# Reading two PSUM banks with one operation: exponentials of one head and row maxima of the other

## The reference, cut to what matters

```python
qkv = (x @ w_qkv.T + b_qkv).reshape(b, n, 3, H, D).transpose(2, 0, 3, 1, 4)
q = _apply_rope(jax.nn.elu(q) + 1.0, sin, cos)
k = _apply_rope(jax.nn.elu(k) + 1.0, sin, cos)
attn = jnp.einsum('bhnd,bhmd->bhnm', q, k) * scale
attn = jax.nn.softmax(attn, axis=-1)
attn_out = jnp.einsum('bhnm,bhmd->bhnd', attn, v)
...
x = _layernorm(x + attn_out + lepe)      # lepe: a depthwise convolution of v along n
h = relu(s0 * concat([x, -x]) @ sign(k0)) * 2
h = relu(s1 * h @ sign(k1)) * 2
x = _layernorm(x + s2 * h @ sign(k2))
```

## Time and profile before

| | us |
|---|---|
| median of 3 runs | 2167.17 |
| lowest and highest | 2163.6 and 2169.74 |
| the profiled execution | 2168.84 |
| its span from first to last instruction | 2166.8 |
| busy in the span: PE, DVE, ACT, POOL | 2077.0, 1696.8, 1499.5, 1008.6 |

### The profile page before, as it was taken

How to read it: one execution, slowest core, us unless ns; L and a number is a source line. 1 busy time by engine, 2 the same in 40 slices (tenths; PEclk the granted TensorE clock), 3 DMA queues, 4 the chain that set the end, 5 groups by cost and what they waited for, 6 DMA issues and landing times.

```text
span 2166.8 us, 43669 instructions
## 1 busy us (share of the span) xinstructions
PE 2077.0 (96%) x17136; PEld 836.7 (39%) x17136; DVE 1696.8 (78%) x3094; ACT 1499.5 (69%) x2867; POOL 1008.6 (47%) x578
## 2 busy tenths in 40 slices
PE   4899999999999999999999999999999999999988
PEld 2123333344433434334343443434343343434345
DVE  7978998787887887878787887878878788877143
ACT  3299888766777667776777767776677766767532
POOL 2849269432866157472584427761475704300000
PEclk8689999999999999999999999999999999999999
DMA  5101200010010200111001200002001110000000
GB/s 179 33 9 37 82 19 26 26 67 21 16 34 20 89 16 9 35 58 49 16 25 26 83 25 17 28 16 96 11 17 36 31 57 16 16 9 28 1 1 39
DMA packets 40428, 76.87 MB, mean 35 GB/s; under 512 B 15024, under 2 KB 19488, under 8 KB 37280
## 3 DMA queue, kind: packets, MB, share of 16 engines
q1 hardware_dynamic: 35040, 51.02, 8.2%
q0 software_dynamic: 5184, 23.07, 2.8%
HBM read 46.27 MB, written 25.17 MB: 33 GB/s over the span
## 4 chain that ended last, share of the span: by engine, by line
PE 79%; DVE 13%; ACT 5%; issue 2%; DMA 0%; POOL 0%; SPq 0%; POOLq 0%; ACTq 0%; DVEq 0%
PE unit_banks L723 25%; PE unit_banks L587 21%; PE o_bank L632 19%; DVE maxima L987 8%; PE unit_banks L736 5%; PE unit_banks L659 4%; ACT probs L814 3%; PE unit_banks L597 2%; PE unit_banks L647 1%; DVE hT L1056 1%; DVE h0T L1059 1%; DVE stats L1133 1%; PE unit_banks L640 0%; ACT work L856 0%; ACT work L855 0%
## 5 line engine op out<-in xcount | busy, mean ns | idle before, releaser
L987 DVE TENSOR_REDUCE maxima<-unit_banks 128x1 f32<-128x512 f32 x2048 | 1307.4, 684 | 326.2 <-PE unit_banks L587 321.3
L814 ACT ACTIVATE probs<-unit_banks 128x512 f32<-128x512 f32 x2048 | 1118.7, 599 | 540.3 <-PE unit_banks L597 536.5
L587 PE MATMUL unit_banks<-k_stack,q_stack 48*128 48x512 f16 x2048 | 660.3, 392 | 26.0 <-DVE maxima L987 22.4
L597 PE MATMUL unit_banks<-q_stack,k_stack 50*128 50x512 f16 x2048 | 657.3, 387 | 6.3 <-ACT probs L814 4.2
L632 PE MATMUL o_bank<-probs,v_pair 128*32 128x256 f32 x8192 | 565.4, 388 | 0.5
L723 PE MATMUL unit_banks<-h0T,w 128*128 128x512 f16 x2048 | 480.1, 380 | 0.0
L1385 POOL TENSOR_TENSOR attn<-o_rows_sb,rden 128x256 f32<-128x256 f32 x63 | 39.2, 622 | 787.9 <-DVE rden L1000 774.3
L587 PEld LDWEIGHTS unit_banks<-k_stack,q_stack 48*128 48x128 f16 x2048 | 155.1, 94 | 525.9 <-DVE maxima L987 273.5
L632 PEld LDWEIGHTS o_bank<-probs,v_pair 128*32 128x32 f32 x8192 | 207.5, 109 | 297.0 <-issue 216.9
L723 PEld LDWEIGHTS unit_banks<-h0T,w 128*128 128x128 f16 x2048 | 189.4, 98 | 222.8 <-issue 33.1
L597 PEld LDWEIGHTS unit_banks<-q_stack,k_stack 50*128 50x128 f16 x2048 | 155.5, 93 | 46.3 <-ACT probs L814 37.0
(11 more groups left out here) (148 smaller groups left out, 1664.0 us busy)
## 6 DMA issues: line engine op xcount, KB each, us to landing
rows<-in_x POOLq DMA_DIRECT2D x8, 1024.0 KB, 5.9
q_stack<-q_scratch SPq DMA_DIRECT2D x128, 64.0 KB, 2.0
k_stack<-k_scratch SPq DMA_DIRECT2D x128, 64.0 KB, 2.0
work<-in_xT SPq DMA_DIRECT2D x7, 1024.0 KB, 6.9
q_scratch<-parts POOLq DMA_DIRECT2D x14, 512.0 KB, 3.3
k_scratch<-parts POOLq DMA_DIRECT2D x14, 512.0 KB, 3.2
out<-rows SPq DMA_DIRECT2D x7, 1024.0 KB, 4.9
q_stack<-q_scratch SPq DMA_DIRECT2D x128, 32.0 KB, 1.9
```

What stands on the lines that cost most here:

```text
L587: nc.tensor.matmul(units.out(unit), q_stack[row:row + STACK, r, t * P:(t + 1) * P], k_stack[row:row + STACK, r, half * 512:(half + 1) * 51 ...
L597: nc.tensor.matmul(units.out(unit), k_stack[row:end, r, kt * P:(kt + 1) * P], q_stack[row:end, r, half * 512:(half + 1) * 512], start=True ...
L814: nc.scalar.activation(probs[:, 2 * (kt % 2) + h, half * 512:(half + 1) * 512], units.out(unit), ACT.Exp, scale=exp_regs[2 * (n % PAIRS) + ...
L987: nc.vector.reduce_max(maxima[:, v // T % 2, h * T + t, half:half + 1], units.out(unit), AXIS_X)\
```

## The change

ACT reads both halves of T(s,1,·) with one exponential of 1024 columns. It waits for the second half to be full, and frees both banks at its end. DVE does the same for the row maxima of S(v,0,·) where the two banks are neighbours in the right order: with the ring (0, 1) that is always so, and with the ring (0, 1, 4) in every third step. The exponentials of head 0 and the row maxima of head 1 stay as they were, and so do the row maxima ahead of the step loop.

```diff
+            def exp_both_halves(s, h):
+                n, kt = divmod(s, T)
+                first, last = (("T", s, h, half) for half in range(2))
+                units.wait_full(act, last)
+                if h == 1:
+                    wait(act, pv_done, 2 * (s - 2) + 2)
+                banks = slice(units.bank[first], units.bank[first] + 2)
+                nc.scalar.activation(probs[:, 2 * (kt % 2) + h], units.psum[:, banks].rearrange("p b n -> p (b n)"), ACT.Exp,
+                                     scale=exp_regs[2 * (n % PAIRS) + h]).then_inc(units.free_sem(first), 2)
...
-                for half in range(2):
-                    exp_probs(s, 1, half)
+                exp_both_halves(s, 1)
...
+            def row_max_both_halves(v, h):
+                t = v % T
+                first, last = (("S", v, h, half) for half in range(2))
+                if units.bank[last] != units.bank[first] + 1:
+                    for half in range(2):
+                        row_max(v, h, half)
+                    return
+                units.wait_full(dve, last)
+                banks = slice(units.bank[first], units.bank[first] + 2)
+                nc.vector.reduce_max(maxima[:, v // T % 2, h * T + t, :], units.psum[:, banks], AXIS_X)\
+                  .then_inc(units.free_sem(first), 2)
...
-                    for half in range(2):
-                        row_max(v, 0, half)
+                    row_max_both_halves(v, 0)
```

## The result

The changed kernel takes 2248.89 us (median of 4 runs, 2245.91 to 2259.46) against 2168.11: a ratio of 1.0385, 95% interval 1.0365 to 1.0404, or 81 us more. I had forecast 2230, range 2188 to 2262. The profiled execution took 2248.41 us with a span of 2246.3, 79.5 us more than before.

What follows compares the result with a forecast made beforehand. PE, busy 96% of the span, was taken to bound the kernel. Batch terms 20.6 + 10.1 + 24 + 3.9 + 4.2 = 62.8 us on 2168.84 gave 2231.6, less 1.7 for the median: 2230, range 2188 to 2262.

Steps and rivals of the forecast that it cites:

- Free steps: Steps without a dealt piece: 3.16 us against 2.49 in the first batch, 3.46 against 2.85 in the second.
- plain L1 steps: Steps with a long dealt piece: gap 2.41 us against the 1.93 needed, so nothing lost.
- the first batch: Its 49 free steps, where the T ring of two banks decides: 20.6 us more.
- Durations: Wide operations of 1024 columns: row maximum 1.22 us (ends 1.15 and 1.37), exponential 1.05 us (0.98 and 1.20).
- The small terms of the third to seventh batch: Scale, hT, L0, elu, V, statistics and bound steps: 4.8 us a batch, 24 for five.
- steps with two L0 units: Third to seventh batch, DVE already late: nine steps, each 0.2 us later, 1.8 us a batch.
- the steps around elu: Third to seventh batch, elu on ACT: cycle 3.46 to 3.97 us, PE's work covering two thirds; eight steps, 1.4 us together.
- V, statistics, bound: Third to seventh batch, where the wide operation's end, 0.15 us later, reaches the next S: 0.7 us a batch.
- The clock: Rival: PE's clock falls in the new free steps, 0.44 us more a cycle, 28 us, 2258; chance 0.15.
- the eighth batch: Six free steps at about 0.35 us, L0 steps 1.8, the rest 0.3: 4.2 us more.
- That saved overhead pays: Rival: fewer, wider operations shorten the ACT and DVE part of the chain, 6 us faster, 2161; chance 0.05.
- Half the price: Rival: ACT's and DVE's lateness already hides more of the free steps' cost; some 30 us, 2199; chance 0.19.

Runs made afterwards that it cites:

- the filled kernel: Changed kernel plus four matmuls on zero weights between the groups in 59 free steps, against the kernel before: 2243.64 us, ratio 1.0354.
- the second filled run: Changed kernel plus four zero-weight matmuls in 59 free steps and in the hT and scale steps, against the kernel before: 2246.3 us, ratio 1.0366.
- the run with the products between: Changed kernel with all products with v between the two groups in free steps, against the kernel before: 2248.08 us, ratio 1.0374.
- the run on long steps: Kernel before with the joining only in steps whose dealt piece is of L1 or L2: 2173.12 us, ratio 1.0026.

## Why the prediction was right, and by how much it was short

**Direction, mechanism, place: right.** The wait that the change adds (a later start and a later release in rings of two banks) is what the time went into. Free steps take 3.13 and 3.48 us where I had 3.16 and 3.46; plain L1 steps are unchanged at a gap of 2.39 us; the first batch came out at 20.8 against 20.6. That last agreement is partly luck: both traces have about 14 us at the lower clock in the first batch, at different steps, and the two losses happen to be alike. After, they are steps 27 to 29, which take 14.65 us where the filled kernel takes 10.56. Before, they are steps 11, 12, 17 and 18, which take 18.91 us, and 15.17 in the changed kernel, with the clock full and with the added wait. Steps 17 and 18 lie in these windows, first before, then after, columns as in the earlier trace rows:

```profile
146.00:156.00 10.00, 9.72 (x68) 2.50 (x64) 5.92 (x11) 8.16 (x16) 0.00 (x0) 0.66 0.01 2
```

```profile
148.00:158.00 10.00, 8.89 (x79) 2.78 (x77) 8.06 (x13) 9.04 (x15) 0.00 (x0) 1.00 0.01 2
```

**Durations: right.** 1.225 and 1.024 us lie inside the ends and next to the values taken.

**The small terms of the third to seventh batch: short.** In the fourth batch, where the clock never fell, by the sums over its steps:

| term | forecast | measured |
|---|---|---|
| scale step | 0.2 | 0.22 |
| both hT steps and the free one behind | 0.7 | 1.05 |
| steps with two L0 units | 1.8 | 1.4 |
| the steps around elu | 1.4 | 1.84 |
| V, statistics, bound | 0.7 | 1.3 |
| sum | 4.8 | 5.8 |

The L0 mechanism was sized right, and not its count (I had nine such steps, the table has eight). Step 87 after, to be held against the earlier trace rows:

```profile
396.49 0.39 PE L587 MATMUL unit_banks<-k_stack,q_stack 48*128 48x512 f16 x1
...
399.32 1.28 DVE L997 TENSOR_REDUCE maxima<-unit_banks 128x1 f32<-128x512 f32 x2
```

From the second S to the next row maxima it is 2.83 us, before 2.63: the 0.2 that I had. But the loss arrives at PE in only five of the eight steps, as 0.2 in four of them and 0.48 in the fifth. The last term was mis-sized most: I had it as an allowance, without naming the steps.

**The clock: I held it for a rival with 28 us, and it was part of the likeliest case with about 9.** The chance that I gave it was for a kernel that stays at 1.2 GHz in its free steps; what came were short stretches, six of them between the first step and the last (two before). The page's clock row has as many slices below 9 as before, three, because a slice is 56 us long. My main argument against this rival was a wrong reading: step 11 before has no gap of about 3 us. Its longest wait of PE is 1.11 us, against 0.91 in step 27 after, behind which the clock falls too, and the lower clock shows in the durations already within that step:

```profile
125.51 0.39 PE L597 MATMUL unit_banks<-q_stack,k_stack 50*128 50x512 f16 x1 [1.11 <-ACT probs L814]
...
127.18 0.61 PE L597 MATMUL unit_banks<-q_stack,k_stack 50*128 50x512 f16 x1
```

After, the fall in the third batch lies in hT step 147 (timeline of PE):

```profile
642.33 0.63 PE L703 MATMUL unit_banks<-ident,rows 128*128 128x128 f32 x4 [1.54 <-DVE rows L1138]
...
643.46 1.93 PE L632 MATMUL o_bank<-probs,v_pair 128*32 128x256 f32 x16
645.32 0.60 PE L587 MATMUL unit_banks<-k_stack,q_stack 48*128 48x512 f16 x1
```

PE waits 1.54 us for DVE, and then the products with v take 1.93 us. In the same step of the fourth batch the wait is the same 1.54, the clock stays, and they take 1.07:

```profile
904.12 0.63 PE L703 MATMUL unit_banks<-ident,rows 128*128 128x128 f32 x4 [1.54 <-DVE rows L1138]
...
905.22 1.07 PE L632 MATMUL o_bank<-probs,v_pair 128*32 128x256 f32 x16
```

I put the share at about 9 us, by an estimate from the durations of steps. In the changed kernel the lower clock costs about 4.1 us in steps 27 to 29, 1.5 in steps 78 and 79 (8.69 against 7.18 in the second filled run), 3.7 in the third, fifth and seventh batch together (each is 1.1 to 1.3 longer than the fourth), 2.2 in the eighth (against the first filled run), and 1.7 after the last T. From these 13 us go the 4 or so that the kernel before loses in steps 11, 12, 17 and 18. The 1.7 us after the last T I had at nothing. The program is the same there, and over the 37 us behind the last T the mean granted clock is 0.95 before and in the run with the products between, whose stretches after the last T are equally long (114.5 us), and 0.91 in the changed kernel (116.1 us):

```profile
2052.00:2089.00 37.00, 30.01 (x194) 17.06 (x194) 21.00 (x53) 13.48 (x24) 4.45 (x8) 0.95 0.00 0
```

```profile
2130.00:2167.00 37.00, 30.01 (x186) 17.24 (x186) 20.30 (x52) 12.80 (x23) 4.43 (x8) 0.91 0.00 0
```

The rest of the 17 us between 62.8 and 79.5 is mostly the small terms (5 in five batches) and the eighth batch (1.5 beside the clock); the second batch without its fall is 14.3 against 14.0. The split is no better than the estimates in it.

**The rivals.** That saved overhead pays fell with the run on long steps: even where joining costs next to nothing it gains nothing, with ACT at 68% and DVE at 77% busy. Of the Trainium skill's two rules that I weighed (Perfetto Trace Analysis, Optimizing Scalar/DVE Operations) the second held here, that an unsaturated engine which causes bubbles elsewhere may do better with its instructions broken up: joined, they cost 81 us. In the trace PE's clock fell in step 147 after a single wait of 1.54 us, and in the fourth batch it stayed up after the same wait. The Trainium skill's rule that names long idle gaps as what brings the clock down (TensorE: Matmul & The Clock Gate, Why this matters for your kernels) does not account for such a fall: by that rule alone it would have stayed up. Half the price fell with the first batch, which took its whole 20.8 us where this rival had about half of 20.6.

## What to carry to other kernels

Before joining operations that read a ring of buffers, measure in the timeline how long the ring's turn takes: late start, whole operation, release, refill, next start. If that turn is longer than the producer's own work between two groups, each joining costs about the difference, however idle the reading engine is; the same operations joined one group later cost 2.8 times as much here. A third buffer buys most of it back, moving the producer's work from one short gap to the other does not, and small allowances for steps where the reader is late should be counted step by step, since they were a third of what this forecast missed.

## What the runs showed of the hardware that I had not expected

One operation over two neighbouring PSUM banks runs at the same rate as over one: 1225 ns for 1024 columns on DVE against 682 for 512, and 1024 ns against 597 on ACT. PE's clock fell in step i = 19 of the third, fifth and seventh batch and not in that of the fourth and sixth (mean 0.79 from 640 to 648 us, 1.00 from 901.3 to 906.3), with the same steps and the same wait of 1.54 us ahead of it, and the runs of the changed kernel differ by 13.5 us. A fall costs time even where PE has no wait: before, step 18 takes 5.00 us with PE busy throughout, and 3.17 in the changed kernel. What makes it fall in one batch and not in the next, these runs do not settle.
